# First cross-attention of a six-block kernel: keys made per tile instead of a key weight folded into the query

## The chip, the cores and the metric

The kernel runs on one NeuronCore of a Trainium2 chip. The metric is the device time of one execution in microseconds (us): the median of three runs of the kernel before is 1192.25 us (1191.71 to 1194.04).

## What is computed

The reference is a chain of six blocks on a residual stream `x` of 16 batches x 64 rows x 256: cross-attention, self-attention, a mixture of experts with its own attention, a second cross-attention, self-attention and a feed-forward network. The change touches the first block alone:

```
x = x + xattn(layernorm(x), ctx)        # ctx: 16 x 256 x 256
lat = layernorm(latents) * w + b        # 16 x 64 x 256
ctx = layernorm(context) * w + b
q = (lat @ Wq) -> 16 heads of 64
k, v = split(ctx @ Wkv) -> 16 heads of 64 each
attn = softmax(clip(q k^T / 8, -11, 11))
out = (attn v) @ Wo + bo
```

## The kernel before

**Tiles.** The block works on 8 tiles `t`. A tile is two batches: 128 rows of `x` and 512 rows of context. Everything of it lives in the class `X0` of SBUF tiles and in the functions `pe_x0`, `act_x0`, `dve_x0` and `pool_x0`, one for each engine, which are written out in program order. There is no planner: each engine runs its list in order, and semaphores (class `C0`) tie the lists together.

**Precision.** A float32 matmul is issued as two passes, each with its own weight load. The large products are instead split: each operand is written as an upper part in fp32r and the rest (`_hi`, `_lo`), and three fp32r products (hi*hi, hi*lo, lo*hi) are summed, for each of the `KD` = 2 halves of the 256 contraction rows. So one "three-product fill" of a bank is 6 matmuls of 128 x 128 weights over 512 columns.

**PSUM.** Banks 0 to 3 are a ring. `FILLS` lists in which order TensorE fills them; fill number n waits until the engine that empties fill n-4 has done so (`wait_bank`). Banks 4 and 5 take the scores in turn, banks 6 and 7 the products with the values.

**One tile on TensorE** (loop at the end of `pe_x0`):
- `fill_v(t, i)`, i = 0 to 7 (L530): the values, a three-product fill each. The even ones are copied to `x0v` by ScalarE (L655), the odd ones by VectorE (L748).
- `scores(t, u)`, u = 0 to 7 (L545): a three-product fill of 128 keys over 512 columns (8 heads x 64 queries), into bank 4 or 5. ScalarE takes the exponential (L659), GpSimd clips it (L823). The clip stands behind the exponential, with exp(-11) and exp(11) as its bounds.
- The scores don't use keys. They use `A`, the query times the transposed key weight: `fill_A(t+1, gr)`, gr = 0 to 3 (L514), 8 float32 matmuls each (16 passes), weights `x0wkT` of 64 rows x 128 columns over 128 columns. Even and odd heads lie in rows 0 to 63 and 64 to 127, and go to two banks. ScalarE writes `A_hi` (L650), VectorE `A_lo` (L742); only then are the two banks free.
- `fill_cT`, `fill_lat` (L464, L471): transposes of the next tile's normalised context and latents. VectorE makes `cT`, `cT_hi` and `cT_lo` of them.
- `fill_q` twice (L484): the next tile's queries, 32 float32 passes in all.
- `values(t, pg)` twice (L563): 64 passes each, behind the clips of their scores. The first waits also for the last copies of `v`.
- `fill_T` twice (L573) and `fill_y` (L583): transposes of the attended rows, and the output product.

**VectorE** also normalises tile t+2 in four parts (`norm`), between which GpSimd makes the reciprocal deviations (L308, L310). GpSimd's list interleaves these with the clips.

**Ahead of the first tile**: `cT`, `lat` and `q` of tile 0, four fills that transpose the key weight (`fill_K`, L496, emptied at L644 and L736 into `x0wkT`), four `fill_A(0, ...)`, and the split of the value weight (L674, L784). The weights' DMAs are issued at the kernel's start by SyncE.

Of the kernel before, what the change touches and what calls it, by code (L numbers as in the profile page):

```python
# [54 lines left out]
def build(nc, a, out):  # L55

    with ExitStack() as ctx:
# [97 lines left out]
        class X0:  # L155
# [14 lines left out]
            wk = nc.alloc_sbuf_tensor_at("x0wk", [P, KD, INNER], F32, offset=at[0])  # L170
# [3 lines left out]
            wkT = sb("x0wkT", [P, 8, D])  # L174
# [225 lines left out]

        class C0:
            fill = sem("c0_fill")
            by_act = sem("c0_by_act")
            by_dve = sem("c0_by_dve")
            A_hi = sem("c0_A_hi")
# [11 lines left out]
            y_add = sem("c0_y_add")  # L417
            x_done = sem("c0_x_done")


        FILLS = [(0, "cT0"), (0, "cT1"), (0, "lat"), (0, "q0"), (0, "q1")] + [(0, f"K{i}") for i in range(4)] + [(0, f"A{g}{par}") for g in range(4) for par in range(2)]
        for t in range(T):
            nxt = t + 1 < T
            FILLS += [(t, f"v{i}") for i in range(4)]
            FILLS += [(t + 1, k) for k in ("cT0", "cT1", "lat") if nxt]
            FILLS += [(t, f"v{i}") for i in range(4, 8)]
            FILLS += [(t + 1, k) for k in ("q0", "q1") if nxt] + [(t, "T0")]
            FILLS += [(t + 1, f"A{g}{par}") for g in range(3) for par in range(2) if nxt] + [(t, "T1")]
            FILLS += [(t + 1, f"A3{par}") for par in range(2) if nxt] + [(t, "y")]
        BY_DVE = ("cT1", "q1", "K1", "K3", "v1", "v3", "v5", "v7", "T1", "y")  # L430
        FILL_AT = {f: n for n, f in enumerate(FILLS)}
        EMPTIED, _of = [], {"act": 0, "dve": 0}
        for _t, _k in FILLS:
            _e = "dve" if _k in BY_DVE or _k[0] == "A" else "act"
            _of[_e] += 1
            EMPTIED.append((_e, _of[_e]))

        def bank_of(t, k):
            return ps[:, FILL_AT[t, k] % 4, :]

        def wait_emptied(eng, t, k):
            by, n = EMPTIED[FILL_AT[t, k]]
            eng.wait_ge(C0.by_act if by == "act" else C0.by_dve, n)

        def wait_filled(eng, t, k):
            eng.wait_ge(C0.fill, FILL_AT[t, k] + 1)

        def wait_bank(pe, t, k):
            n = FILL_AT[t, k] - 4
            if n >= 0:  # L450
                wait_emptied(pe, *FILLS[n])

        S_BANK, PV_BANK = (4, 5), 6

        def pe_x0(pe):
            g = X0

            def fill_cT(t, i):
                if i == 0:
                    pe.wait_ge(ln_done, 2 * t + 2)  # L460
                wait_bank(pe, t, f"cT{i}")
                dst = bank_of(t, f"cT{i}")
                for tok in range(4):
                    last = nc.tensor.transpose(dst[:, tok * P:tok * P + P], g.cn[:, tok, i * P:i * P + P], ident)  # L464
                last.then_inc(C0.fill, 1)

            def fill_lat(t):
                wait_bank(pe, t, "lat")
                dst = bank_of(t, "lat")
                for i in range(KD):  # L470
                    last = nc.tensor.transpose(dst[:, i * P:i * P + P], g.lat[:, i * P:i * P + P], ident)  # L471
                last.then_inc(C0.fill, 1)

            def fill_q(t, i):
                if i == 0:
                    if t == 0:
                        pe.wait_ge(ld["x0q"], 16)
                    wait_emptied(pe, t, "lat")
                wait_bank(pe, t, f"q{i}")
                dst = bank_of(t, f"q{i}")  # L480
                for j in range(4):
                    for k in range(KD):
                        at_w = (4 * i + j) * P
                        last = nc.tensor.matmul(dst[:, j * P:j * P + P], g.wq[:, k, at_w:at_w + P], g.latT[:, k, :],  # L484
                                                start=(k == 0), stop=(k == KD - 1))
                last.then_inc(C0.fill, 1)

            def fill_K(i):
                if i == 0:
                    pe.wait_ge(ld["x0k"], 16)  # L490
                wait_bank(pe, 0, f"K{i}")
                dst = bank_of(0, f"K{i}")
                for j in range(2):
                    for k in range(KD):
                        at_w = (2 * i + j) * P
                        last = nc.tensor.transpose(dst[:, (2 * j + k) * P:(2 * j + k) * P + P], g.wk[:, k, at_w:at_w + P], ident)  # L496
                last.then_inc(C0.fill, 1)

            def fill_A(t, gr):

                pg, kc = divmod(gr, KD)
                if gr == 0:
                    if t == 0:
                        wait_emptied(pe, 0, "K2")
                        wait_emptied(pe, 0, "K3")
                    wait_emptied(pe, t, "q0")
                if gr == 2:
                    wait_emptied(pe, t, "q1")
                for par in range(2):
                    wait_bank(pe, t, f"A{gr}{par}")  # L510
                for j in range(4):
                    for par in range(2):
                        r = slice(64 * par, 64 * par + 64)
                        last = nc.tensor.matmul(bank_of(t, f"A{gr}{par}")[:, j * P:j * P + P], g.wkT[r, 4 * pg + j, kc * P:kc * P + P],  # L514
                                                g.qT[r, 4 * pg + j, :], start=True, stop=True)
                        if j == 3:
                            last.then_inc(C0.fill, 1)

            def fill_v(t, i):
                tok, half = i // 2, i % 2  # L520
# [4 lines left out]
                wait_bank(pe, t, f"v{i}")  # L525
                dst = bank_of(t, f"v{i}")
                hi, lo = g.cT_hi[t % 2], g.cT_lo[t % 2]
                for k in range(KD):
                    for n, (m, w) in enumerate(((hi, g.wv_hi), (hi, g.wv_lo), (lo, g.wv_hi))):
                        last = nc.tensor.matmul(dst, m[:, k, tok * P:tok * P + P], w[:, k, half * 512:half * 512 + 512],  # L530
                                                start=(k == 0 and n == 0), stop=(k == KD - 1 and n == 2))
                last.then_inc(C0.fill, 1)

            def scores(t, u):
                pg, b, kt = u // 4, u // 2 % 2, u % 2
                if u % 4 == 0:
                    for gr in (2 * pg, 2 * pg + 1):
                        wait_emptied(pe, t, f"A{gr}1")
                if 8 * t + u > 1:
                    pe.wait_ge(C0.exp, 8 * t + u - 1)  # L540
                hi, lo = g.cT_hi[t % 2], g.cT_lo[t % 2]
                keys = slice((2 * b + kt) * P, (2 * b + kt) * P + P)
                for k in range(KD):
                    for n, (w, m) in enumerate(((hi, g.A_hi), (hi, g.A_lo), (lo, g.A_hi))):
                        last = nc.tensor.matmul(ps[:, S_BANK[u % 2], :], w[:, k, keys], m[:, k, b, pg, :, :, :].rearrange("p a j n -> p (a j n)"),  # L545
                                                start=(k == 0 and n == 0), stop=(k == KD - 1 and n == 2))
                last.then_inc(C0.scores, 1)

            def values(t, pg):
                pe.wait_ge(C0.clip, 8 * t + 4 * pg + 4)  # L550
                if 2 * t + pg > 0:
                    pe.wait_ge(C0.att, 2 * t + pg)
# [38 lines left out]
            for i in range(4):  # L591
                fill_K(i)
# [1979 lines left out]
```

## Time and profile before

| | |
|---|---|
| median of 3 runs | 1192.25 us |
| profiled execution | 1198.49 us |
| its span (first to last instruction) | 1196.8 us |
| start to first `fill_v` | 37.84 us |
| tile 0 | 42.97 us |
| tiles 1 to 6 | 42.3 us each |
| tile 7 | 35.16 us |
| the rest | 827.13 us |
| TensorE busy over the span | 88% |

The profiled execution is 6.2 us slower than the median. Times below are read from it, counted from the first instruction of the span.

### The profile page before, as it was taken

What the parts mean: (1) busy time and instruction counts of PE and PEld (TensorE: products, weight loads), DVE (VectorE), ACT (ScalarE), POOL (GpSimd) and SP (SyncE); (2) the same over time, 40 slices, a digit from 0 to 9 for tenths busy, and PEclk for the clock granted to TensorE, in tenths of its full rate; (3) what the DMA queues carried; (4) which work ended last, traced back from release to release, by engine and by line L of the source; (5) the groups of instructions that cost most, each with busy time, mean ns of one, the idle gap of its engine ahead of it and who ended that gap; (6) DMA issues with size and microseconds to landing.
All of it is one profiled execution on the core that took longest, in us unless ns stands there. A gap on an engine that the chain in (4) does not pass through costs nothing.

```text
span 1196.8 us, 27530 instructions
## 1 busy us (share of the span) xinstructions
PE 1058.3 (88%) x11715; PEld 911.5 (76%) x11715; DVE 643.6 (54%) x1374; ACT 477.7 (40%) x868; POOL 241.9 (20%) x381
## 2 busy tenths in 40 slices
PE   3899999999996889999659999996999987997998
PEld 3778888888875777777549999984787866775787
DVE  3745445454323344555577999973666651344342
ACT  1433232332322544454236677751433332443332
POOL 2211211211111112232432444424100000010000
PEclk9999999999998788888559999996999997997999
DMA  9200000000004300000064665713101002000000
GB/s 304 74 19 19 18 2 19 1 1 1 1 1 170 139 2 11 11 11 11 10 194 137 211 237 201 246 55 110 50 22 35 2 2 62 3 2 1 1 18 18
DMA packets 55672, 72.79 MB, mean 61 GB/s; under 512 B 8504, under 2 KB 48896, under 8 KB 54912
## 3 DMA queue, kind: packets, MB, share of 16 engines
q1 hardware_dynamic: 54016, 66.85, 16.8%
q0 software_dynamic: 1536, 4.20, 1.1%
q8 instruction: 93, 1.52, 0.5%
q14 instruction: 27, 0.22, 0.1%
HBM read 60.02 MB, written 11.01 MB: 59 GB/s over the span
## 4 chain that ended last, share of the span: by engine, by line
PE 73%; DVE 16%; ACT 5%; issue 3%; POOL 2%; DMA 1%; DVEq 0%; SPq 0%; ACTq 0%; POOLq 0%
PE ps L1993 7%; PE ps L2011 7%; PE ps L545 6%; PE ps L530 5%; PE ps L2253 5%; PE ps L1408 4%; PE ps L1009 3%; PE ps L563 3%; PE ps L1370 3%; PE ps L484 3%; PE ps L583 2%; PE ps L1336 2%; PE ps L514 2%; PE ps L946 2%; PE ps L1319 2%
## 5 line engine op out<-in xcount | busy, mean ns | idle before, releaser
L368 POOL TENSOR_TENSOR rn_tmp<-rn_cur,eps 128x1 f32<-128x1 f32 x48 | 13.4, 279 | 516.3 <-DVE rn_cur L362 516.3
L659 ACT ACTIVATE x0pT<-ps 128x512 f32<-128x512 f32 x64 | 38.3, 599 | 120.6 <-PE ps L545 120.6
L1993 PE MATMUL ps<-moe_xT_hi,ew_1hi 128*128 128x256 f32 x240 | 69.5, 289 | 3.9 <-DVE moe_xT_lo L2137 3.9
L2011 PE MATMUL ps<-ew_2hi,eh_hi 128*128 128x256 f32 x240 | 69.3, 289 | 1.2 <-DVE eh_lo L2145 1.2
L1993 PE MATMUL ps<-moe_xT_lo,ew_1hi 128*128 128x256 f32 x240 | 68.9, 287 | 0.0
L1993 PE MATMUL ps<-moe_xT_hi,ew_1lo 128*128 128x256 f32 x240 | 68.8, 287 | 0.0
L2143 DVE CAST eh_hi<-eh 128x512 fp32r<-128x512 f32 x60 | 61.0, 1017 | 14.0 <-ACT eh L2054 13.9
L2011 PE MATMUL ps<-ew_2hi,eh_lo 128*128 128x256 f32 x240 | 67.3, 281 | 0.0
L2011 PE MATMUL ps<-ew_2lo,eh_hi 128*128 128x256 f32 x240 | 67.3, 280 | 0.0
L823 POOL TENSOR_SCALAR x0pT<-x0pT 128x512 f32<-128x512 f32 x64 | 39.4, 616 | 104.9 <-ACT x0pT L659 103.2
L2253 PE MATMUL ps<-f,ffw 128*128 128x512 f32 x256 | 59.3, 391 | 0.3 <-DVE f L2324 0.3
L748 DVE COPY x0v<-ps 128x512 f32<-128x512 f32 x32 | 22.1, 691 | 69.2 <-PE ps L530 69.2
L2145 DVE TENSOR_TENSOR eh_lo<-eh,eh_hi 128x512 fp32r<-128x512 f32 x60 | 58.1, 969 | 2.1
L1408 PEld LDWEIGHTS ps<-sa_v,sa_pT 64*64 64x64 f32 x1536 | 48.6, 138 | 13.7 <-ACT sa_pT L1576 12.7
L2253 PEld LDWEIGHTS ps<-f,ffw 128*128 128x128 f32 x256 | 47.8, 188 | 10.9 <-DVE f L2324 1.1
L1408 PE MATMUL ps<-sa_v,sa_pT 64*64 64x18 f32 x1536 | 51.0, 211 | 5.1 <-ACT sa_pT L1576 2.4
L530 PE MATMUL ps<-x0wv_hi,x0cT_hi 128*128 128x512 f32 x128 | 52.8, 413 | 0.6 <-DVE x0A_lo L742 0.6
L742 DVE TENSOR_TENSOR x0A_lo<-ps,x0A_hi 128x512 fp32r<-128x512 f32 x64 | 40.5, 685 | 22.8 <-ACT x0A_hi L650 22.8
L1958 POOL TENSOR_TENSOR ew_1lo<-ew,ew_1hi 128x1024 fp32r<-128x1024 f32 x15 | 39.0, 2602 | 64.6 <-ACT ew_1hi L1948 64.6
L545 PE MATMUL ps<-x0A_hi,x0cT_hi 128*128 128x512 f32 x128 | 51.3, 401 | 0.0
L530 PE MATMUL ps<-x0wv_hi,x0cT_lo 128*128 128x512 f32 x128 | 50.6, 395 | 0.0
L545 PE MATMUL ps<-x0A_lo,x0cT_hi 128*128 128x512 f32 x128 | 50.5, 395 | 0.0
(324 smaller groups left out, 2872.3 us busy)
## 6 DMA issues: line engine op xcount, KB each, us to landing
ew<-L_ffn_W_dram SPq DMA_DIRECT2D x30, 1024.0 KB, 7.5
x0cin<-ctx_dram SPq DMA_DIRECT2D x8, 512.0 KB, 4.2
x1cin<-ctx_dram SPq DMA_DIRECT2D x8, 512.0 KB
xg<-moe_in SPq DMA_DIRECT2D x15, 256.0 KB, 7.8
moe_out<-moe_y SPq DMA_DIRECT2D x15, 256.0 KB, 7.8
moe_in<-padneg SPq DMA_DIRECT2D x3, 1024.0 KB, 12.9
maskrow<-mask_BxS_ik_dram SPq DMA_DIRECT2D x2, 1024.0 KB, 8.5
x0wq<-L_xattn_Wq_dram SPq DMA_DIRECT2D x1, 1024.0 KB, 7.5
```

Of the source, the lines that this page charges most:

```text
L530: last = nc.tensor.matmul(dst, m[:, k, tok * P:tok * P + P], w[:, k, half * 512:half * 512 + 512], start=(k == 0 and n == 0), stop=(k == K ...
L545: last = nc.tensor.matmul(ps[:, S_BANK[u % 2], :], w[:, k, keys], m[:, k, b, pg, :, :, :].rearrange("p a j n -> p (a j n)"), start=(k == 0 ...
L659: nc.scalar.activation(g.pT[:, u, :], ps[:, S_BANK[u % 2], :], ACT.Exp, scale=64.0 ** -0.5).then_inc(C0.exp, 1)
L742: nc.vector.tensor_tensor(g.A_lo[:, kc, :, pg, par, :, :].rearrange("p b j n -> p j b n"), bank_of(t, f"A{gr}{par}").rearrange("p (j b n) ...
L823: nc.gpsimd.tensor_scalar(g.pT[:, u, :], g.pT[:, u, :], high, low, ALU.min, ALU.max).then_inc(C0.clip, 1)
L1408: last = nc.tensor.matmul(RS.bank(n, "pv")[rows_b, hd * XVW:hd * XVW + XVW], g.pT[rows_b, r, at_p:at_p + N], g.v[n % 2][rows_b, hd, :], st ...
L1958: nc.gpsimd.tensor_tensor(lo, w, hi.bitcast(F32), ALU.subtract).then_inc(MO.w_lo_pool, 1)
L1993: last = nc.tensor.matmul(ps[:, n % 3, j * BT:j * BT + BT], w[b % 2][:, i, f * P:f * P + P], v[b % 2][:, i, :], start=(i == 0 and m == 0), ...
L2011: last = nc.tensor.matmul(ps[:, O_BANK[b % 2] + c, 0:D], v[n % 3][:, j * BT + c * P:j * BT + c * P + P], w[b % 2][:, f, :], start=(f == 0 ...
L2143: nc.vector.tensor_copy(eh_hi[n % 3][:, :], eh[n % 3][:, :]).then_inc(MO.hi, 1)
L2145: nc.vector.tensor_tensor(eh_lo[n % 3][:, :], eh[n % 3][:, :], eh_hi[n % 3][:, :].bitcast(F32), ALU.subtract).then_inc(MO.split, 1)
L2253: last = nc.tensor.matmul(ps[:, 2 + f % 4, :], w[:, k, f * P:f * P + P], src[part][:, k, :], start=(k == 0 and part == 0), stop=(k == ks - ...
```

## The change

The key weight is no longer transposed and multiplied into the query. Its upper and lower parts are made once, and the keys of each tile are made as eight three-product fills `K0` to `K7` of the ring, one for each pair of heads, emptied into `x0kT` by ScalarE (even) and VectorE (odd). The scores are then float32 matmuls over the 64 rows of one head: 128 keys as weights, 64 queries as moving columns, 16 matmuls for one `scores(t, u)`, even heads into bank 4 and odd heads into bank 5. There are four `scores(t, u)` a tile instead of eight. The exponential and the clip work on both banks in one instruction of 128 x 1024. The order on all engines changes: `K` and `q` of the next tile lie between the last `v` fills, the two `values`, the two `T` and `y`. The ring is now an instance `R0` of the class `Ring`, which the second cross-attention used already.

```
-            A_hi = sb("x0A_hi", [P, KD, 2, 2, 2, 4, N], F32R)
-            A_lo = sb("x0A_lo", [P, KD, 2, 2, 2, 4, N], F32R)
+            kT = sb("x0kT", [P, 8, 512])
-            pT = sb("x0pT", [P, 8, 512])
+            pT = sb("x0pT", [P, 4, 2, 512])
...
+        X0_FILLS = [(0, k) for k in ("cT0", "cT1", "lat", "q0", "q1")] + [(0, f"K{i}") for i in range(8)]
         for t in range(T):
...
+            X0_FILLS += [(t, f"v{i}") for i in range(4)] + [(t + 1, "cT0"), (t + 1, "cT1")] * nxt
+            X0_FILLS += [(t, "v4"), (t, "v5")] + [(t + 1, "lat")] * nxt + [(t, "v6"), (t, "v7")]
+            X0_FILLS += [(t + 1, k) for k in ("K0", "q0", "K1", "K2", "q1", "K3") if nxt] + [(t, "T0")]
+            X0_FILLS += [(t + 1, k) for k in ("K4", "K5") if nxt] + [(t, "T1")] + [(t + 1, k) for k in ("K6", "K7") if nxt] + [(t, "y")]
+        S0, PV0 = ps[:, 4:6, :], ps[:, 6:8, :]
...
+            def fill_K(t, i):
+                if i == 0:
+                    pe.wait_ge(C0.cT_lo, t + 1)
+                    if t == 0:
+                        pe.wait_ge(C0.w_lo, KD)
+                R0.wait_free(pe, t, f"K{i}")
+                hi, lo = g.cT_hi[t % 2], g.cT_lo[t % 2]
+                for k in range(KD):
+                    for n, (w, m) in enumerate(((g.wk_hi, hi), (g.wk_hi, lo), (g.wk_lo, hi))):
+                        last = nc.tensor.matmul(R0.bank(t, f"K{i}"), w[:, k, i * P:i * P + P], m[:, k, :],
+                                                start=(k == 0 and n == 0), stop=(k == KD - 1 and n == 2))
+                last.then_inc(C0.fill, 1)
...
             def scores(t, u):
+                b = u // 2
+                if u == 0:
+                    for k in ("q0", "q1", "K6", "K7"):
+                        R0.wait_emptied(pe, t, k)
+                if 4 * t + u > 0:
+                    pe.wait_ge(C0.exp, 4 * t + u)
+                for j in range(8):
+                    for par in range(2):
+                        r = slice(64 * par, 64 * par + 64)
+                        last = nc.tensor.matmul(S0[:, par, j * N:j * N + N], g.kT[r, j, u * P:u * P + P], g.qT[r, j, b * N:b * N + N], start=True, stop=True)
                 last.then_inc(C0.scores, 1)
...
             for t in range(T):
                 nxt = t + 1 < T
...
+                scores(t, 0)
+                fill_v(t, 0)
+                fill_v(t, 1)
+                scores(t, 1)
+                fill_v(t, 2)
+                fill_v(t, 3)
                 if nxt:
                     fill_cT(t + 1, 0)
                     fill_cT(t + 1, 1)
+                scores(t, 2)
+                fill_v(t, 4)
+                fill_v(t, 5)
+                if nxt:
                     fill_lat(t + 1)
...
+                scores(t, 3)
+                fill_v(t, 6)
+                fill_v(t, 7)
                 if nxt:
+                    fill_K(t + 1, 0)
                     fill_q(t + 1, 0)
+                values(t, 0)
+                if nxt:
+                    fill_K(t + 1, 1)
+                    fill_K(t + 1, 2)
                     fill_q(t + 1, 1)
+                values(t, 1)
+                if nxt:
+                    fill_K(t + 1, 3)
                 fill_T(t, 0)
                 if nxt:
+                    fill_K(t + 1, 4)
+                    fill_K(t + 1, 5)
                 fill_T(t, 1)
                 if nxt:
+                    fill_K(t + 1, 6)
+                    fill_K(t + 1, 7)
                 fill_y(t)
...
             def exp(t, u):
+                act.wait_ge(C0.scores, 4 * t + u + 1)
+                if u == 0 and t > 0:
+                    act.wait_ge(C0.pv, 2 * t)
+                nc.scalar.activation(g.pT[:, u, :, :], S0[:, :, :], ACT.Exp, scale=64.0 ** -0.5).then_inc(C0.exp, 1)
...
+            act.wait_ge(ld["x0k"], 16)
+            for i in range(KD):
+                upper(g.wk, g.wk_hi, i)
+            K(0, 0)
+            K(0, 2)
...
             cT(0)
             q(0)
+            for i in range(KD):
+                lower(g.wk, g.wk_hi, g.wk_lo, i, i + 1)
+            K(0, 1)
+            K(0, 3)
+            lower(g.wv, g.wv_hi, g.wv_lo, 0, KD + 1)
+            K(0, 5)
+            lower(g.wv, g.wv_hi, g.wv_lo, 1, KD + 2)
+            K(0, 7)
             for part in range(4):
                 norm(1, part)
```

`values(t, 0)` now waits for all four clips of its tile. `upper` and `lower` are a copy on ScalarE and a subtraction on VectorE of 128 x 1024, as those of the value weight were. Ahead of tile 0 the order on TensorE is `cT`, `lat`, `q0`, `q1`, `K0` to `K7`.

## Rows read from the trace of the kernel before

**Rows 1.** The page's first line: busy us, share, instructions of each engine.

```profile
PE 1058.3 (88%) x11715; PEld 911.5 (76%) x11715; DVE 643.6 (54%) x1374; ACT 477.7 (40%) x868; POOL 241.9 (20%) x381
```

**Rows 2.** Busy us (x instructions) in four stretches; then PEclk, DMA share, GB/s.

```profile
0.00:37.84 37.84, 15.20 (x123) 14.16 (x123) 16.43 (x39) 10.06 (x17) 6.63 (x13) 1.00 0.87 283
...
123.09:165.38 42.29, 40.24 (x356) 34.26 (x355) 20.54 (x43) 14.00 (x25) 7.92 (x15) 1.00 0.04 14
...
334.51:369.67 35.16, 31.44 (x249) 25.39 (x247) 6.72 (x13) 7.68 (x13) 5.78 (x11) 1.00 0.00 0
369.67:1196.80 827.13, 729.55 (x8867) 631.92 (x8867) 476.90 (x1023) 361.43 (x663) 174.87 (x255) 0.89 0.22 71
```

**Rows 3.** Groups by shape, 0 to 380 us: busy us, mean ns, idle before.

```profile
L823 POOL TENSOR_SCALAR x0pT<-x0pT 128x512 f32<-128x512 f32 x64 | 39.4, 616 | 104.9 <-ACT x0pT L659 103.2
L659 ACT ACTIVATE x0pT<-ps 128x512 f32<-128x512 f32 x64 | 38.3, 599 | 120.6 <-PE ps L545 120.6
...
L784 DVE TENSOR_TENSOR x0wv_lo<-x0wv,x0wv_hi 128x1024 fp32r<-128x1024 f32 x2 | 2.4, 1220 | 0.1
L674 ACT ACTIVATE x0wv_hi<-x0wv 128x1024 fp32r<-128x1024 f32 x2 | 2.1, 1068 | 0.0
```

**Rows 4.** Chain that ended last, tile 2: start us, us, engine, tile, line.

```profile
123.09 1.39 PE ps L530 x6
...
134.24 0.89 PE ps L464 x8
...
145.95 2.09 PE ps L563 x64
148.04 1.59 PE ps L545 x6
149.63 3.57 PE ps L484 x32
153.20 0.44 PE ps L573 x4
...
158.50 1.90 DVE x0A_lo L742 x3
...
160.53 1.16 PE ps L514 x16
161.70 3.68 PE ps L583 x16
```

**Rows 5.** Timeline of the weight loads, four places: start us, us, form, count.

```profile
156.68 1.86 PEld L514 LDWEIGHTS ps<-x0qT,x0wkT 64*128 64x128 f32 x32
...
421.44 0.98 PEld L1370 LDWEIGHTS ps<-sa_kT,sa_qbd 32*128 32x128 f32 x32
...
454.01 0.23 PEld L1394 LDWEIGHTS ps<-sa_qbd,sa_kT 32*64 32x64 f32 x16
454.42 0.52 PEld L1438 LDWEIGHTS ps<-wg,sa_mT 128*128 128x128 f32 x4 [0.17 <-issue]
```

**Rows 6.** Timeline of VectorE ahead of tile 0.

```profile
27.71 0.69 DVE L732 COPY x0qT<-ps 128x512 f32<-128x512 f32 x1 [5.59 <-PE ps L484]
```

**Rows 7.** Chain that ended last, tile 7.

```profile
355.44 0.70 DVE x0v L748
...
358.37 1.60 PE ps L545 x6
...
369.67 0.43 DVE x_res L766
```

**Rows 8.** Timeline of tile 2: VectorE at cT1, GpSimd's second rstd.

```profile
135.15 0.81 DVE L723 TENSOR_SCALAR x0cT<-ps,col 128x512 f32<-128x512 f32 x1 [1.58 <-PE ps L464]
...
144.60 0.55 POOL L310 TENSOR_TENSOR ln_rs<-ln_ve,neghalf 128x1 f32<-128x1 f32 x1
```

**Rows 9.** Busy time by stretches, behind two pauses of TensorE; columns as in Rows 2.

```profile
371.70:374.50 2.80, 0.00 (x0) 0.00 (x0) 1.61 (x13) 0.00 (x0) 1.76 (x9) 0.51 0.03 6
...
407.50:416.00 8.50, 8.43 (x57) 7.30 (x58) 3.70 (x10) 3.09 (x7) 0.99 (x4) 0.50 0.01 2
```

More of the change, by code:

```diff
@@ L391, in row_apply, with __init__, bank, wait_emptied @@
             last.then_inc(rn_done, 1)
+        class Ring:
+            def __init__(self, banks, fills, by_dve, fill, by_act_sem, by_dve_sem, more_by_dve=()):
+                self.banks, self.fills, self.fill = banks, fills, fill
+                self.at = {f: n for n, f in enumerate(fills)}
+                self.emptied, of = [], {"act": 0, "dve": 0}
+                for t, k in fills:
+                    e = "dve" if k in by_dve or (t, k) in more_by_dve else "act"
+                    of[e] += 1
+                    self.emptied.append((by_act_sem if e == "act" else by_dve_sem, of[e]))
+            def bank(self, t, k):
+                return self.banks[self.at[t, k] % len(self.banks)]
+            def wait_emptied(self, eng, t, k):
+                eng.wait_ge(*self.emptied[self.at[t, k]])
+            def wait_filled(self, eng, t, k):
+                eng.wait_ge(self.fill, self.at[t, k] + 1)
+            def wait_free(self, pe, t, k):
+                n = self.at[t, k] - len(self.banks)
+                if n >= 0:
+                    pe.wait_ge(*self.emptied[n])
         class C0:
@@ L430, in build @@
[L430 to L443, printed above, removed]
@@ L455, in pe_x0 @@
+            X0_FILLS += [(t + 1, k) for k in ("K4", "K5") if nxt] + [(t, "T1")] + [(t + 1, k) for k in ("K6", "K7") if nxt] + [(t, "y")]
+        R0 = Ring([ps[:, i, :] for i in range(4)], X0_FILLS, ("cT1", "q1", "K1", "K3", "K5", "K7", "v1", "v3", "v5", "v7", "T1", "y"), C0.fill, C0.by_act, C0.by_dve)
+        S0, PV0 = ps[:, 4:6, :], ps[:, 6:8, :]
         def pe_x0(pe):
@@ L483, in fill_q @@
                         at_w = (4 * i + j) * P
-                        last = nc.tensor.matmul(dst[:, j * P:j * P + P], g.wq[:, k, at_w:at_w + P], g.latT[:, k, :],
+                        last = nc.tensor.matmul(R0.bank(t, f"q{i}")[:, j * P:j * P + P], g.wq[:, k, at_w:at_w + P], g.latT[:, k, :],
                                                 start=(k == 0), stop=(k == KD - 1))
                 last.then_inc(C0.fill, 1)
[L488 to L520, printed above, removed]
+            def fill_K(t, i):
                 if i == 0:
@@ L529, in fill_v @@
                     for n, (m, w) in enumerate(((hi, g.wv_hi), (hi, g.wv_lo), (lo, g.wv_hi))):
-                        last = nc.tensor.matmul(dst, m[:, k, tok * P:tok * P + P], w[:, k, half * 512:half * 512 + 512],
+                        last = nc.tensor.matmul(R0.bank(t, f"v{i}"), m[:, k, tok * P:tok * P + P], w[:, k, half * 512:half * 512 + 512],
                                                 start=(k == 0 and n == 0), stop=(k == KD - 1 and n == 2))
@@ L534, in scores @@
             def scores(t, u):
[L535 to L546, printed above, removed]
+                b = u // 2
[8 more added lines that the diff above has]
+                        last = nc.tensor.matmul(S0[:, par, j * N:j * N + N], g.kT[r, j, u * P:u * P + P], g.qT[r, j, b * N:b * N + N], start=True, stop=True)
                 last.then_inc(C0.scores, 1)
             def values(t, pg):
-                pe.wait_ge(C0.clip, 8 * t + 4 * pg + 4)
+                if pg == 0:
+                    pe.wait_ge(C0.clip, 4 * t + 4)
+                    R0.wait_emptied(pe, t, "v6")
+                    R0.wait_emptied(pe, t, "v7")
+                    if t == 0:
+                        pe.wait_ge(C0.ones, 1)
                 if 2 * t + pg > 0:
                     pe.wait_ge(C0.att, 2 * t + pg)
-                if pg == 0:
-                    wait_emptied(pe, t, "v6")
-                    wait_emptied(pe, t, "v7")
-                    if t == 0:
-                        pe.wait_ge(C0.ones, 1)
                 for par in range(2):
@@ L590, in pe_x0 @@
             fill_q(0, 1)
-            for i in range(4):
-                fill_K(i)
-            for gr in range(4):
-                fill_A(0, gr)
+            for i in range(8):
+                fill_K(0, i)
             for t in range(T):
                 nxt = t + 1 < T
-                for i in range(4):
-                    fill_v(t, i)
-                    scores(t, i)
+                scores(t, 0)
[4 more added lines that the diff above has]
+                fill_v(t, 3)
                 if nxt:
@@ L638, in q @@
             def q(t):
[L639 to L651 removed]
+                R0.wait_filled(act, t, "q0")
@@ L828, in pool_x0 @@
             for t in range(T):
[L829 removed]
+                for u in range(4):
                     clip(t, u)
[L831 removed]
+                    if u == 1 and t + 2 < T:
                         ln_rstd_pool(pool, 5, 2 * t + 4)
[L833 removed]
+                    if u == 2 and t + 2 < T:
                         ln_rstd_pool(pool, 1, 2 * t + 5)
                 row_rstd(pool, t, t % 2, "mla", t)
[L841 to L863 removed]
         class C1:
```

224 lines of the change are left out of this document (77 added, 147 removed).

## The prediction

> **What bounds the kernel now.** The page's first line comes first [rows 1]: TensorE is busy 88% of the span, the next engine 54%. The view by stretches says where that holds [rows 2]: the first cross-attention ends at 369.67 us, and within it a tile of 42.29 us has 40.24 us of TensorE, 20.54 of VectorE, 14.00 of ScalarE and 7.92 of GpSimd, at a granted clock of 1.00. So this block is bound by TensorE, and in it a us less for another engine is worth nothing unless TensorE waits for it. The chain of tile 2 shows what TensorE's 42.29 us are [rows 4]: sixteen fills of v and scores at 1.39 (22.3), two entries into such a fill after another form (1.59 instead of 1.39: 0.4), cT and lat 0.89, two `values` (2.09 and about 2.02), q 3.57, two T at 0.44, four fills of A (1.16 for one that stands alone, 2.06 for two together, 1.09 where `values` follow: 4.3), y 3.68. That is 40.1. The other 2.2 are waits: about 0.9 ahead of the first `values`, which start at 145.95 where the fills end at 145.05 (134.24 + 0.89 + seven fills + one entry), and 1.3 in the A chain, where each group of two banks must pass ScalarE and then VectorE (1.90 of x0A_lo stands in the chain) before T1 and A3 get a bank.
>
> **The change part by part.**
>
> *K instead of scores.* Eight three-product fills of K per tile take the place of eight of scores: the same 6 matmuls of 128x128 weights over 512 columns. 11.1 us a tile out, 11.1 in: nothing.
>
> *The new scores instead of A.* A was 32 float32 matmuls a tile, 64 passes; the new scores are 64 matmuls, 128 passes, of half the columns (64 instead of 128). Counted by moved columns the two are equal. Counted by weight loads the new ones are double, and I take the loads. The reasons are four rows of the weight-load timeline [rows 5]. (a) Full array, 128 columns of weights, only 8 moving columns: (0.52 - 0.19)/3 = 0.110 us from load to load. Eight columns cannot take that, so it is the load's price. (b) Row groups of 32 rows, 128 columns, 64 moving columns: (0.98 - 0.19)/31 = 0.0256, a quarter of (a). The columns alone would allow half of that: the row of A, (1.86 - 0.19)/31 = 0.054 for 128 moving columns in two row groups, bounds a pass of 128 columns at 0.108 per row group, so one of 64 at 0.054 and, over four groups, 0.0135. So each row group pays about 0.10 for a load and the groups overlap. (c) Groups of 32 rows with 64 columns of weights: 16 loads start within 0.23 - 0.14 = 0.09 us, so there is no fixed floor of 0.025 per instruction that would explain (b). (d) The new scores have two row groups and 128 columns of weights: 0.107/2, or 0.054 a pass, which is what A's row shows too, where load and columns tie. One `scores(t, u)` is 32 x 0.054 = 1.73, and 0.3 to enter (A alone: 1.16 for 16 passes of 0.054): 2.03. Four: 8.1 a tile. Bounds: from below the columns alone, 0.027 a pass, 1.16 a call, 4.6 a tile; from above the full-array spacing of (a) with no overlap, 3.8 a call, 15.3 a tile. I take 2.03, since A's form has the same weights (64 rows x 128 columns, alternating in the same way between two banks), and it is the nearest row.
>
> The Trainium skill, "TensorE: Matmul & The Clock Gate", section "LDWEIGHTS (loading the stationary operand)", says that a weight load is timed by its columns and not by its rows, about 107 ns for 128 columns; by it the sum stays as it is, and it speaks against this change, because half the rows make no load cheaper. The same page (section "Wait — 56ns, not 53.3ns?") has a start-to-start floor of about 25 ns for small matmuls; were (b) that floor and not the load, the sum would be the first rival's. Rows 5 (c) speak against it here.
>
> *Entries.* Fills of six now follow another form at K1, K3, K4 and K6, four instead of two, 0.19 each: +0.4. What follows scores is in their 0.3.
>
> *The waits.* The A chain is gone, 1.3 saved. K's banks are emptied by one copy each (0.60 or 0.69), and between each K and the fill that needs its bank lie three other fills; T1 follows the attended rows by 4.7 us of PE work: no wait. The first `values` now stand behind v7, K0 and q0, 3.2 us, so v7's copy (0.2 to start and 0.70 [rows 7]) is hidden. What is late next is the last clip, since GpSimd runs it behind the second deviation. From the start of VectorE's cT to the end of that deviation are 145.15 - 135.15 = 10.0 us [rows 8]; cT starts 0.2 after cT1 is filled, and the clip is twice 0.62 [rows 3]: 11.4 after cT1. TensorE gets to `values` after two scores, four v, lat, K0 and q0: 4.1 + 5.6 + 0.2 + 1.4 + 1.8 = 13.1. Hidden, by 1.7; if the scores took 1.16, it would be late by about 0.1 to 0.5. All of the 2.2 goes. The single pair of score banks waits for the exponential: 0.2 + about 1.07 (a ScalarE instruction of 1024, [rows 3]) against 2.8 of v fills: hidden.
>
> *Tile.* 42.3 - 4.3 + 8.1 + 0.4 - 2.2 = 44.3 us, +2.0.
>
> *Ahead of tile 0.* q1 is filled at 27.7, its copy ends at 28.4 [rows 6], and then VectorE makes the two lower parts of the key weight, about 1.2 each [rows 3], so the first K can start at 31.1 (ScalarE's upper parts, 2.1 from 25.4 on, lie beside it; the weight has long landed). The eight K end at 42.2. In TensorE's pause of 3.4 us the clock is at risk: pauses of 5 and 3 us elsewhere brought the granted clock down to 0.50, and once it stayed there for 8.5 us of work [rows 9]; the shorter pauses here did not. Between 0 and 4.3 us, I take 1.8 (half of some 4 us of work at half clock). Then K7's copy, 1.0: the first scores start at 45.0. Before, v started at 37.84 [rows 2]. The split of the value weight and norm(1) lie beside K and the first v fills: nothing.
>
> *Tile 7* has no K and no q. Scores 8.1, v 11.2 and one entry 0.2; then the tail of before without its last scores fill: 369.67 - 355.44 - 1.60 [rows 7] = 12.6 less the 0.3 that lies beside `values`: 12.3. That is 31.8, against 35.2.
>
> *Sum.* 45.0 + 7 x 44.3 + 31.8 = 386.9 for the end of the block, against 369.67: +17.2 us. What follows is untouched: 827.13. The profiled span would be 1214.0 and its execution 1215.7; with the same distance to the median (1198.49 to 1192.25) that is 1209.4 us.
>
> **The rivals.**
>
> *The loads are hidden, the columns bound the scores (0.027 a pass).* Faster: each call is 0.87 cheaper, 32 of them 27.8; the clip then shows for up to 0.5 in six tiles, 3 back. 17.2 - 24.8 = -7.6: 1184.6 us. It turns at 0.037 us a pass, where the 32 calls cost 2.03 - 17.2/32 = 1.5 each. For it: no row has 64-row weights with 64 moving columns, and A's 0.054 can be the columns' alone. Against it: (a) with (b), a quarter of the columns' and loads' time at four groups, where the columns allow an eighth. Chance 0.11.
>
> *The clock falls inside the tiles.* Scores are short passes, with the array half idle behind loads; if the clock went to half for 4 us of each tile, each loses 2 us, 16 in all: 1225 us. For it: in the self-attention, stretches of such passes are followed by a granted clock of 0.50 too (its second stretch in [rows 9] begins so). Against it: every tile of before holds 4 us of `values` and 4 of A at a clock of 1.00, and the new scores stand between dense fills. Chance 0.08.
>
> *No overlap of the two row groups:* 3.8 a call, +56: 1265 us. A's row is against it. Chance 0.02.
>
> *The change moves work and no time:* the scores at about 0.037 a pass, gain and loss level: 1192 us. It needs a load of seven tenths of its price. Chance 0.04.
>
> **How the numbers follow.** My forecast has 0.75: 1209.4 us, its own range 1203 to 1216 (scores 1.85 to 2.2 a call, clock 0 to 4.3, and about 3 us either way for where the clock's changes fall in the untouched 827 us, whose mean clock is 0.89 [rows 2]). For 8 in 10 the range reaches a little towards both sides: 1199 to 1222. A change under 0.2% (2.4 us) can't be told from none. Faster 0.11, same 0.04, slower 0.85.
>
> **What would show it.** In the profile after: 32 weight loads of 64x128 in one `scores` spanning about 1.9 us, 0.054 apart (right), or 0.9 us (the first rival). A tile of 44.3 us, with TensorE busy nearly all of it and no wait at `values` above 0.1. The first K at 31.1 us, at a granted clock under 1.00 for some us; the first scores at 43 to 46. The end of `y` of tile 7 at 383 to 391. The forecast is wrong if a tile takes less than 42.3 us, and its reasons are wrong if a tile is longer for waits and not for scores.

## The result, and the profile after

The changed kernel takes 1208.93 us (median of four runs, 1205.67 to 1211.16); the kernel before, with one more run, takes 1193.14. The ratio is 1.0131, with a 95% interval of 1.0104 to 1.0159: slower by 1.3%. A second comparison (experiment six) gave 1.0107 (1.009 to 1.0123). The forecast was 1209.4 us, with the block 17.2 us longer.

The profiled execution took 1205.67 us, the fastest of the four. The stretches of its profile are cut at its own tiles, columns as in [rows 2]: the part ahead of tile 0, tiles 0, 1 and 2, and what lies behind the block.

```profile
0.00:40.50 40.50, 19.31 (x91) 16.32 (x91) 16.89 (x38) 9.54 (x13) 6.63 (x13) 1.00 0.81 265
40.50:84.85 44.35, 44.35 (x420) 37.89 (x420) 22.38 (x53) 11.69 (x17) 8.41 (x12) 1.00 0.08 25
84.85:129.20 44.35, 44.35 (x421) 37.87 (x422) 18.53 (x40) 11.68 (x17) 7.16 (x11) 1.00 0.04 13
129.20:173.50 44.30, 44.30 (x420) 37.83 (x422) 18.55 (x40) 11.68 (x17) 7.16 (x11) 1.00 0.04 14
...
382.80:1203.90 821.10, 726.49 (x8867) 629.81 (x8867) 477.90 (x1023) 361.39 (x663) 174.66 (x255) 0.90 0.22 72
```

A tile went from 42.29 [rows 2] to 44.3 us, and TensorE, which was idle for 2.05 us of the old tile, is now busy for all of it. VectorE has 2.0 us a tile less to do, ScalarE 2.3, GpSimd 0.8: all of that is worth nothing here, since TensorE is never idle in the tile. The chain that ended last, in tile 2 of the kernel after, holds TensorE alone (start us, us, engine, tile, line; L521 the scores, L506 v, L463 the transposes of the context, L494 K, L481 q, L538 `values`, L547 T, L557 y):

```profile
129.15 1.93 PE ps L521 x32
131.08 3.00 PE ps L506 x12
...
139.00 0.87 PE ps L463 x8
...
149.93 1.40 PE ps L494 x6
151.33 1.78 PE ps L481 x16
153.12 2.02 PE ps L538 x64
155.13 2.99 PE ps L494 x12
158.12 1.78 PE ps L481 x16
159.91 2.02 PE ps L538 x64
161.93 1.59 PE ps L494 x6
163.52 0.44 PE ps L547 x4
163.96 2.81 PE ps L494 x12
...
169.99 3.45 PE ps L557 x16
```

Compare [rows 4]: the first `values` followed a wait and T1 and A3 stood behind VectorE's x0A_lo. None of those waits is left, and nothing has come in their place. What costs is the first line, four times a tile. The weight loads of one call of the scores:

```profile
134.00 1.86 PEld L521 LDWEIGHTS ps<-x0qT,x0kT 64*128 64x128 f32 x32 [0.36 <-issue]
```

(1.86 - 0.19)/31 = 0.054 us from load to load, although each pass moves only 64 columns. (0.19 is the recorded length of one load of 128 columns; the rest, over 31, is the distance from load to load.) That is to the digit the row of A [rows 5], whose passes moved 128.

### The profile page after: what moved, and what is told of

Same layout as the page of the kernel before. It is cut to its first block, busy times and chain, and to the rows that moved or that the text cites. A ratio compares the mean times of both kernels' runs of the same rounds, so it can differ in the third digit from the quotient of the medians.

```text
span 1203.9 us, 28359 instructions
## 1 busy us (share of the span) xinstructions
PE 1084.8 (90%) x12211; PEld 934.8 (78%) x12211; DVE 629.3 (52%) x1342; ACT 459.8 (38%) x804; POOL 235.6 (20%) x349
## 4 chain that ended last, share of the span: by engine, by line
PE 79%; DVE 12%; ACT 4%; issue 3%; DMA 1%; POOL 1%; SPq 0%; DVEq 0%; ACTq 0%; POOLq 0%
PE ps L506 8%; PE ps L494 8%; PE ps L1945 6%; PE ps L1963 6%; PE ps L521 5%; PE ps L2205 5%; PE ps L1360 4%; PE ps L961 3%; PE ps L538 3%; PE ps L481 3%; PE ps L557 2%; PE ps L1322 2%; PE ps L1288 2%; PE ps L898 2%; PE ps L1271 2%
## 5 line engine op out<-in xcount | busy, mean ns | idle before, releaser
L367 POOL TENSOR_TENSOR rn_tmp<-rn_cur,eps 128x1 f32<-128x1 f32 x48 | 13.4, 280 | 572.2 <-DVE rn_cur L361 572.2
L640 ACT ACTIVATE x0pT<-ps 128x1024 f32<-128x1024 f32 x32 | 32.9, 1027 | 93.6 <-PE ps L521 93.6
L521 PEld LDWEIGHTS ps<-x0qT,x0kT 64*128 64x128 f32 x1024 | 59.7, 188 | 9.6 <-issue 9.6
L521 PE MATMUL ps<-x0qT,x0kT 64*128 64x64 f32 x1024 | 64.1, 275 | 0.9 <-DVE x0kT L719 0.9
L1360 PEld LDWEIGHTS ps<-sa_v,sa_pT 64*64 64x64 f32 x1536 | 49.6, 141 | 13.1 <-ACT sa_pT L1528 12.7
L494 PE MATMUL ps<-x0cT_hi,x0wk_hi 128*128 128x512 f32 x128 | 53.3, 416 | 3.1 <-issue 3.1
L506 PE MATMUL ps<-x0wv_hi,x0cT_hi 128*128 128x512 f32 x128 | 54.0, 422 | 0.0
L1945 PEld LDWEIGHTS ps<-moe_xT_hi,ew_1hi 128*128 128x128 f32 x240 | 47.2, 197 | 5.5 <-DVE moe_xT_lo L2089 5.4
L494 PE MATMUL ps<-x0cT_hi,x0wk_lo 128*128 128x512 f32 x128 | 50.6, 396 | 0.0
## 6 DMA issues: line engine op xcount, KB each, us to landing
moe_in<-padneg SPq DMA_DIRECT2D x3, 1024.0 KB, 12.7
```

Source lines behind the costliest of these rows:

```text
L494: last = nc.tensor.matmul(R0.bank(t, f"K{i}"), w[:, k, i * P:i * P + P], m[:, k, :], start=(k == 0 and n == 0), stop=(k == KD - 1 and n == 2))
L506: last = nc.tensor.matmul(R0.bank(t, f"v{i}"), m[:, k, tok * P:tok * P + P], w[:, k, half * 512:half * 512 + 512], start=(k == 0 and n == ...
L521: last = nc.tensor.matmul(S0[:, par, j * N:j * N + N], g.kT[r, j, u * P:u * P + P], g.qT[r, j, b * N:b * N + N], start=True, stop=True)
L1360: last = nc.tensor.matmul(RS.bank(n, "pv")[rows_b, hd * XVW:hd * XVW + XVW], g.pT[rows_b, r, at_p:at_p + N], g.v[n % 2][rows_b, hd, :], st ...
L1945: last = nc.tensor.matmul(ps[:, n % 3, j * BT:j * BT + BT], w[b % 2][:, i, f * P:f * P + P], v[b % 2][:, i, :], start=(i == 0 and m == 0), ...
```

## The experiments

**One: half the moving columns.** The kernel after, with

```
+                n_q = N if 4 * t + u == 0 else N // 2
...
-                        last = nc.tensor.matmul(S0[:, par, j * N:j * N + N], ..., g.qT[r, j, b * N:b * N + N], start=True, stop=True)
+                        last = nc.tensor.matmul(S0[:, par, j * N:j * N + n_q], ..., g.qT[r, j, b * N:b * N + n_q], start=True, stop=True)
```

> The changed kernel, but every call of the scores after the very first multiplies only the first 32 of 64 query columns of each head (the other half of the score bank keeps what the first call wrote, so half of the scores are left out). The 32 weight loads of a call stay. Theory (a call is bound by its float32 weight loads, 0.107 us each in each of two row groups, 0.054 a pass): a call stays at 1.9 us and a tile at 44.3. Rival, columns bound the call: a pass falls from 0.054 to about 0.027, a call from 1.93 to about 1.1, a tile to about 41.

The half that is not multiplied keeps what the first call wrote, so this kernel leaves out half of the scores. Its chain in tile 2, the first two calls of scores (L522) and the v fills between:

```profile
130.39 1.91 PE ps L522 x32
132.29 3.00 PE ps L506 x12
135.29 1.91 PE ps L522 x32
```

1.91 us for 1.93, and a tile of 44.16 (130.39 to 174.55). Half of the columns are worth 0.02 us: the columns don't bound the call. That throws out the first rival as it was written.

**Two: one row group after the other.**

```
-                for j in range(8):
-                    for par in range(2):
+                for par in range(2):
+                    for j in range(8):
```

> The changed kernel with the two loops of the scores exchanged: all eight even heads (rows 0 to 63) first, then all eight odd ones (rows 64 to 127). Same 32 passes, loads and columns. Theory (a load takes 0.107 us in its row group and two groups overlap): without alternation there is no overlap, 0.107 a pass, a call of 3.4 to 3.7 us, a tile of about 51 us, +55 us in all. Rival, each pass has a fixed price of 0.054 whatever its row group (an issue or port limit): the call stays at 1.9.

Loads of one call in the timeline, and a stretch that holds the second call of tile 2 (151.20 to 154.61) with v fills on both sides:

```profile
144.83 3.25 PEld L521 LDWEIGHTS ps<-x0qT,x0kT 64*128 64x128 f32 x32 [0.33 <-issue]
```

```profile
150.00:158.00 8.00, 8.00 (x47) 6.66 (x46) 1.68 (x4) 1.97 (x3) 1.45 (x2) 0.79 0.01 2
```

(3.25 - 0.19)/31 = 0.099 us a load instead of 0.054, a call of 3.32 us in the chain, the block's end at 447.1 for 382.8 and one run of 1278.13 us. So there is no fixed price of 0.054 per pass; alternating rows 0 to 63 with rows 64 to 127 is what nearly halves it. The call is a little under the 3.4 that were expected, and the block grows by 64 us where +55 was expected. Four longer calls are 5.6 us a tile. Another 1.5 come from the clock: TensorE is busy without a gap, and yet the granted clock falls, a mean of 0.79 in the second row, and the two v fills behind the second call take 4.43 us for 2.99. In two of the eight tiles it falls twice. The kernel after has 1.00 in every tile shown.

**Three: four tiles of the array.**

```
-                        last = nc.tensor.matmul(S0[:, par, j * N:j * N + N], g.kT[r, j, u * P:u * P + P], g.qT[r, j, b * N:b * N + N], start=True, stop=True)
+                        for c in range(2):
+                            r, keys = slice(64 * par, 64 * par + 64), u * P + 64 * c
+                            last = nc.tensor.matmul(S0[64 * c:64 * c + 64, par, j * N:j * N + N], g.kT[r, j, keys:keys + 64], g.qT[r, j, b * N:b * N + N],
+                                                    start=True, stop=True, skip_group_check=True)
```

> The changed kernel with each weight block of 64 rows x 128 keys cut into two of 64 x 64, which write partitions 0 to 63 and 64 to 127: four tiles of the array, 64 passes a call instead of 32, each with half the weight columns and the same 64 moving columns. Theory: a load of 64 columns takes 0.053 us and four tiles overlap, 64 x 0.053 / 4 = 0.86 and 0.3 to enter, 1.15 us a call instead of 1.93; a tile of about 41.2 us plus up to 0.5 of wait for the last clip; the kernel at 1181 to 1190 us, just faster than before. First rival, an issue floor of about 0.026 a pass: 64 passes are 1.65, a call 1.9, no change (1209). Second rival, each pass costs its row group 0.108 whatever it loads: 64 passes over four tiles are 1.73, no change either.

Loads of one call in its timeline:

```profile
128.02 1.02 PEld L522 LDWEIGHTS ps<-x0qT,x0kT 64*64 64x64 f32 x64 [0.36 <-issue]
```

Its chain, from the scores at the start of tile 2 to those at the start of tile 3:

```profile
124.00 1.09 PE ps L522 x64
125.09 3.00 PE ps L506 x12
128.09 1.09 PE ps L522 x64
...
164.93 1.09 PE ps L522 x64
```

Twice the passes in little more than half the time: 64 loads at (1.02 - 0.14)/63 = 0.014 us, a call of 1.09, a tile of 40.93 and a block that ends at 357.5. The kernel is 0.9906 (0.9884 to 0.9928) of the one before. Both rivals said "no change" and fall: there is no floor of 0.026 per pass, and a row group does not pay 0.108 whatever it loads.

The spacing fell to a quarter, but the edit changes two things, the weight columns of a load and the number of array tiles in turn, and 64 moving columns would by [rows 5]'s working bound a pass at 0.0135 too. So by itself this run does not show what a load of 64 columns costs. A row of the kernel before does: the `values` of the self-attention, 64x64 weights that alternate between two tiles of the array and move only 18 columns, at a granted clock of 1.00:

```profile
401.92 1.94 PEld L1408 LDWEIGHTS ps<-sa_v,sa_pT 64*64 64x64 f32 x64 [0.52 <-ACT sa_pT L1576]
```

(1.94 - 0.14)/63 = 0.029, or 0.057 for each of the two tiles, against 0.054 and 0.108 for 128 columns in two row groups. Half of the columns cost about half, and over four tiles 0.057 gives the 0.014 measured here. The wait for the last clip, expected for up to 0.5, did not appear in this tile; it did in tile 0, with 0.4.

**Four: the kernel before, in another order.** The order on TensorE between the last scores of a tile and y (ScalarE's, VectorE's and the ring's lists follow it):

```
-                    if i == 7:
-                        values(t, 0)
                     scores(t, i)
...
+                values(t, 0)
                 if nxt:
                     fill_A(t + 1, 0)
+                    fill_A(t + 1, 1)
                 values(t, 1)
+                fill_T(t, 0)
                 if nxt:
-                    fill_A(t + 1, 1)
                     fill_A(t + 1, 2)
                 fill_T(t, 1)
                 if nxt:
+                    fill_v(t + 1, 0)
                     fill_A(t + 1, 3)
                 fill_y(t)
```

> The kernel before (key weight folded into the query, wide scores) with another order only: the first values call moved behind the last scores and q, A0 and A1 between the two values calls, the first v fill of the next tile between T1 and A3, and y after A3. No instruction is added or removed. Theory (of a tile's 42.3 us, 2.2 are waits for v7's copy and for the A chain through ScalarE and VectorE): a tile of 40.0 to 40.6, seven tiles, so 12 to 16 us off: 1177 to 1181 us. Rival (the waits only move, VectorE's A_lo and the attended rows come late elsewhere): a tile of 41.5 to 42.3, 1187 to 1193.

In its chain the next tile's transposes begin at 129.01 and, a tile later, here (L465; the tile before ran into L546, scores):

```profile
129.01 0.87 PE ps L465 x8
...
144.82 2.02 PE ps L564 x64
146.84 1.99 PE ps L515 x32
148.83 2.02 PE ps L564 x64
150.84 0.59 PE ps L574 x4
151.43 1.09 PE ps L515 x16
...
169.17 0.87 PE ps L465 x8
```

A tile of 40.16 us, 2.1 less than before, and a block end of 352.5: nearly all of the 2.2 us of waits are gone for no instruction at all (A3's loads still wait 0.5, its matmuls 0.12). The ratio of 0.989 (0.9871 to 0.9909) is a smaller gain than the 17 us of the block, 1.4%, ask for; 1.5 of the 17 are an earlier end of q ahead of tile 0 (26.15 for 27.67), which is not the order's. The rest is taken up below.

**Five: the kernel before, profiled again.**

> The kernel before, unchanged, profiled on the chip on which the others of this call run. Theory (the block alone changed): its block ends at 369 to 370 us as on the first chip, and what differs between the chips and the kernels behind the block (827 us in the first profile, 833 to 834 in those of the third and fourth experiment) is the clock's: 830 to 836 us here. Rival (something behind the block depends on how the block is written): about 827 here, with 833 again for the others.

Block end 369.3, rest 1196.7 - 369.3 = 827.4 us: not the 830 to 836 that were expected. It could not test that expectation as it was meant, since experiments five to eight ran on another chip than one to four. It shows something else. Its start is faster than in the first profile (q ends at 25.17 for 27.67), and then its granted clock falls, with the same short gaps of TensorE (0.83, 1.23 and 1.41 us) that left it at 1.00 in the first profile. The chain at the last A fill, the first v and the first scores, and a stretch of it:

```profile
33.60 2.08 PE ps L514 x16
35.68 2.86 PE ps L530 x6
38.53 2.18 PE ps L545 x6
```

```profile
36.00:38.00 2.00, 2.00 (x6) 1.52 (x6) 1.69 (x4) 0.77 (x2) 0.00 (x0) 0.50 0.03 8
```

They took 1.16, 1.64 and 1.39 in the first profile. So the kernel before can lose about 2 us to the clock ahead of its own tile 0.

**Six: the changed kernel again.**

> The changed kernel, unchanged, on the same chip and in the same rounds as the kernel before. Theory: the block is 13 us longer (382.8 for 369.7), nothing else is changed, so the ratio to the kernel before is 1.011 (1.009 to 1.013). Rival (the change costs something behind the block too): 1.013 to 1.016, as the first comparison's middle of 1.0131 had it.

1.0107 (1.009 to 1.0123), the 1.011 that was expected; 12.7 us between the medians. Behind the block its profile has 824.4 us for the 827.4 of the fifth, so nothing is shown to be lost there. But the reason given for 1.011, a block that is 13 us longer, does not hold as a fixed number: here the block ends at 384.8, 15.6 after the fifth's. What moves is the start. Counted from the end of q ahead of tile 0, the block takes 357.7 us in both profiles of the changed kernel (25.09 to 382.78 and 27.16 to 384.83), and 342.0 and 344.1 in those of the kernel before (27.67 to 369.65 and 25.17 to 369.27), the longer one being that with the slow clock. So the change costs 15.7 us of block where the kernel before keeps its clock, and 13.6 where it loses it.

**Seven: four tiles, and the key weight split earlier.**

```
             lat(0)
-            q(0)
             act.wait_ge(ld["x0k"], 16)
             for i in range(KD):
                 upper(g.wk, g.wk_hi, i)
+            q(0)
```

and the same on VectorE (`lower` twice, then q).

> Four tiles of 64x64 weights for the scores, as in the third experiment, and ahead of tile 0 the split of the key weight on ScalarE and VectorE moved before their copies of q, so that it lies beside TensorE's q. Theory: the first K starts when q ends (25 us) instead of 3.1 us later, everything behind follows: block end at about 354.5 for 357.5, the kernel at 0.988 of the one before. Rival (the pause is given back, since K0 then waits for the copies of the transposed context or the lower part is late all the same): 0 to 1 us, 0.9906 again.

Ahead of tile 0 its chain has no gap between q and K any more:

```profile
19.87 5.41 PE ps L481 x32
25.27 11.22 PE ps L494 x48
```

The block ends at 354.0, the ratio is 0.9868 (0.985 to 0.9886), 1184.15 us for 1199.92: the forecast of this run held. Tile 0 takes 42.2 us (37.35 to 79.58) for the others' 40.9: TensorE waits 0.33 us for the next tile's normalised rows and 0.42 for the last clip before the first `values`. The first rival's arithmetic had such a wait in six tiles; it shows in this one, where VectorE's `norm` begins late, and in the next tile there is none.

**Eight: the early split alone** (the edit of the seventh without that of the third).

> The changed kernel with the early split of the key weight alone. Theory: first K at 25 instead of 28.2, block end 379.7 instead of 382.8. It also shows what the pause of 3.1 us did to the clock: if the pause left it untouched, the eight K fills take 11.4 us with it and 11.2 to 11.4 without.

K starts at 26.00 as q ends (q took 6.20 us here, 5.51 in the kernel after), the eight fills take 11.22 us, the block ends at 380.4 for 382.8. With the pause of 3.1 us they took 11.45 in the kernel after, at a granted clock of 1.00: that pause did not slow the clock.

**Nine: a longer pause at the same place** (the kernel after, and on VectorE):

```
             cT(0)
             q(0)
+            dve.wait_ge(C0.cT_lo, 1)
+            for i in range(5):
+                nc.vector.tensor_copy(g.cn[:, :, :].rearrange("p a b -> p (a b)"), g.cT[:, :, :].rearrange("p a b -> p (a b)")).then_inc(C0.extra, 1)
+                dve.wait_ge(C0.extra, i + 1)
```

> The changed kernel with five extra copies of 128 x 1024 on VectorE between its copy of q and the split of the key weight (their output is not used): TensorE's pause ahead of the first K grows from 3.1 to about 7 us. Theory (the pause of 3.1 us was too short for this place, but the clock does fall in a longer one, as it did behind the block): the granted clock reads 0.50 at the first K, the eight K fills take 13 to 16 us instead of 11.4, the block ends 6 to 8 us later. Rival (here the clock does not fall at all): the K fills stay at 11.4, the block ends later by the pause alone, about 4 us.

Its stretches ahead of and at the first K:

```profile
28.00:30.00 2.00, 0.00 (x0) 0.00 (x0) 1.91 (x3) 0.00 (x0) 0.00 (x0) 1.00 0.97 301
30.00:32.00 2.00, 0.00 (x0) 0.00 (x0) 1.95 (x3) 0.00 (x0) 0.00 (x0) 0.78 1.05 354
32.00:34.00 2.00, 0.80 (x2) 0.73 (x3) 1.10 (x1) 0.00 (x0) 0.00 (x0) 0.50 1.08 352
34.00:36.00 2.00, 2.00 (x6) 1.52 (x6) 0.00 (x0) 0.00 (x0) 0.00 (x0) 0.50 0.17 53
```

A pause of 6.74 us, a granted clock of 0.50 when K begins, and K fills of 13.61 us instead of 11.45: the clock costs 2.2 us. The block ends at 390.0, 7.2 later than in the first profile: 3.6 of pause, 2.2 of clock, 1.4 of a later start.

**Ten: norm(1) between the copies of K** (against the seventh, on VectorE):

```
             K(0, 1)
+            norm(1, 0)
             K(0, 3)
             lower(g.wv, g.wv_hi, g.wv_lo, 0, KD + 1)
+            norm(1, 1)
             K(0, 5)
             lower(g.wv, g.wv_hi, g.wv_lo, 1, KD + 2)
+            norm(1, 2)
             K(0, 7)
-            for part in range(4):
-                norm(1, part)
+            norm(1, 3)
```

> Four tiles and early split, and VectorE's four parts of norm(1) laid between its copies of K1, K3, K5 and K7 instead of behind them. Theory: tile 0, which took 42.1 us for the others' 40.9 since its chain through VectorE and GpSimd begins late, takes 41 to 41.3, minus 1 us: block end about 353, ratio 0.986. Rival: the K copies are delayed and K's fills wait for banks, 0 to 1 us later.

Tile 0 does fall to 41.0 us (40.05 to 81.06), but the first scores wait 2.50 us for K's copies where the seventh experiment's wait 0.87. From the end of q to tile 1 it is 54.7 us against 54.3. The rival was right: the wait moved. The block ends at 355.4 where 353 was expected, and the ratio, 0.9896 (0.9873 to 0.9918), is above the 0.986 expected; its interval overlaps the seventh's (0.985 to 0.9886).

**Eleven: the reordered kernel again, beside the tenth.**

> The reordered kernel with the folded key weight again, in the same rounds as the best version with four tiles. Theory: block end 352.5 as in the fourth experiment, 17 us under the kernel before, and nothing else changed: ratio 0.986, equal to the other within the interval. Rival (part of its gain is given back behind the block, as the first ratio of 0.989 and a rest of 833.9 us seemed to say): 0.989 again, with a rest above 830 us.

0.9855 (0.9828 to 0.9882), 1177.57 us for 1193.64, the block's end at 352.1: the theory held. Its rest is 1176.9 - 352.1 = 824.8 us, and the same kernel's was 833.9 in the fourth experiment. Nine us lie between two profiles of the same code, and they are spread over it. The first matmuls of the second cross-attention, in the fourth experiment and in this one:

```profile
794.03 1.94 PE L915 MATMUL ps<-cst,x1cin 128*128 128x128 f32 x8 [5.49 <-DMA x1cin<-ctx_dram]
```

```profile
787.90 1.94 PE L915 MATMUL ps<-cst,x1cin 128*128 128x128 f32 x8 [5.54 <-DMA x1cin<-ctx_dram]
```

They come 441.6 and 435.8 us behind the end of the block, so 5.8 of the nine us lie ahead of them and 3.4 behind. Over all profiles the rests lie between 821 and 835 us: 827.1 and 827.4 for the kernel before, 821.1 and 824.4 for the one after, without a pattern by version. There is one by chip: 829.3 to 834.5 in experiments one to four, 824.4 to 828.2 in five to eight, 823.7 to 825.4 in nine to eleven. Whether the chip decides it or something else in an execution was not tried; the mean clock of the rest is 0.88 to 0.90 throughout. It is why a change in the block of some 15 us is read well from the chain and worse from the total.

## Why the prediction was right, and where not

**The main step holds.** The new scores are bound by weight loads of two row groups, 0.054 a pass: 1.86 us of loads a call as worked out. This was only argued before, from four forms none of which was the new one. Experiment one shows that columns don't bound, two that the row groups share the time, three with the row of `sa_v` that half the weight columns about halve it. The first rival is refuted, and so is the fixed floor that would have stood for it: 64 loads at 0.014 us. The prediction thought that its row (c) spoke against the floor; it does not. The loads of (c) are recorded as starting within 0.09 us, but here are the matmuls of the same passes, and the next ones:

```profile
454.02 0.47 PE L1394 MATMUL ps<-sa_qbd,sa_kT 32*64 32x128 f32 x16
454.42 0.61 PE L1438 MATMUL ps<-wg,sa_mT 128*128 128x8 f32 x4
```

0.40 us for 16 is 0.025 a pass. A floor of that size was open until experiment three.

**The waits.** All 2.2 us of them are gone, none took their place: right, and experiment four, which changes the order alone, shows that they were real (2.1 us). The change spends that gain and 2 us more.

**The tile.** 44.35 and 44.30 for 44.3. Two terms in it were off and cancel. A call is 1.93, not 2.03, but the fill behind it takes 0.2 more (3.00 for two that are 2.79 elsewhere), and I had both in 2.03: four times 0.1 too little. And y took 3.45 for the 3.68 [rows 4] that I carried over. It then follows K instead of A; that the predecessor is the reason was not tried.

**Ahead of tile 0.** Forecast 45.0, measured 40.50 (and 42.56 in experiment six). This is the step that was mis-sized. The clock's term of 1.8 was zero: a pause of 3.1 us did not bring the clock down, one of 6.7 did (experiment nine), and eight shows K fills within 0.2 us of each other with and without the pause. The risk that [rows 9] showed was real, but the length of one pause does not decide it: of the two pauses behind that working, "5 and 3 us", the second is 2.53 us long (405.04 to 407.57) and did bring the clock to 0.50, and "the shorter pauses here did not" is true of the first profile only (experiment five). The rest of the difference, 2.6 us, is that q ended at 25.1 instead of 27.6, a number carried over from one profile of the kernel before. 1.4 of it is the load of the first constants, `col`, which landed after 4.02 us instead of 5.40; over the profiles it takes 4.0 to 5.8. 1.2 is q itself, 5.51 for 6.70; it takes 5.31 to 6.70, at a clock of 1.00, and why was not tried. The change touches the code of neither.

**Tile 7.** 32.15 us (350.63 to 382.78) for 31.8.

**The sum.** In the first pair of profiles the block grew by 13.1 us, not by 17.2. Tiles 0 to 6 gave 13.5 (forecast 13.4), the last tile took 3.0 off (3.4), and the start gave 2.7 instead of 7.2. Of that miss of 4.5, 2.6 is the earlier q, which belongs to the execution: counted from the end of q the block grew by 15.7, and the forecast without its clock term says 15.4. The medians differ by 15.8 and 12.7 us in the two comparisons, as the 15.7 and the 13.6 of the two pairs of profiles do, though one profile of each kernel cannot show that all executions were like it. That 1208.93 lies so near 1209.4 is partly luck: the forecast had 1.8 too much for the clock, and it expected the profiled execution at 1215.7 where it took 1205.67, 4.1 less in the block and 6.0 less behind it. The distance from that execution to the median was carried over as -6.2 and was +3.3. The range and the direction were right for the reasons given; 1209.4 to within half a us was more than these reasons can promise.

**The clock inside the tiles.** That rival did not come true for this change: 1.00 in each tile. It is a real mechanism close by, though: with loads that are not shared between row groups (experiment two) the granted clock had a mean of 0.79 in a stretch of 8 us inside the block, with TensorE busy all through.

**Which version is best.** Two beat both kernels. The changed one with four tiles and an early split (experiment seven) is 0.9868 (0.985 to 0.9886) of the kernel before. The old one reordered is 0.989 (0.9871 to 0.9909) and 0.9855 (0.9828 to 0.9882) on two chips; its block ends at 352.1 to 352.5, that of the seventh at 354.0. The two are not told apart by the ratios.

## What to carry to other kernels

Price a small float32 matmul by its weight load as well as by its moving columns, take the larger of the two, and divide by the number of row and column tiles of the array that consecutive instructions alternate between. In the forms measured here (64 or 128 weight columns, two or four tiles) this came out to within a tenth. If the load is the larger, try cutting the weights into narrower column tiles: here one cut took a call from 1.93 to 1.09 us. When a change both removes waits and adds work on the bound engine, try the removal alone first: here an order of the same instructions took the gain that the new algebra had spent. And read a change of 1% from the chain of its own stage, counted from a point behind the stage's start: between two executions of one kernel that start moved by 2 us and the rest of the kernel by up to 9.

## What the runs showed of the hardware that was not expected

Four 64x64 tiles of the array in turn took 64 float32 weight loads at 0.014 us each, and their matmuls with them: 1.09 us a call. The 0.0256 in [rows 5], for groups of 32 rows with 128 weight columns, is therefore no floor for every form.

In one row group alone the loads came at 0.099 us, not at the 0.107 to 0.110 that two row groups in turn and the full array give. The group changes once within the 32, but even if that one distance were nothing, the other thirty would be at 3.06/30 = 0.102, so it does not account for the difference, which stays open.

The granted clock of TensorE followed no single pause here. It went to 0.50 in the tiles of experiment two with TensorE busy throughout. It went there behind short gaps of 0.83 to 1.41 us in one execution of the kernel before, and stayed at 1.00 in another. And it stayed at 1.00 in a pause of 3.10 us, though it fell in one of 2.53 us elsewhere in the kernel.
